# Query columns inside the z product, and a new order of the passes, in a gated cross-attention block

## What is computed

```python
# xattn(q=layernorm(x), k=ctx, v=ctx): channel mixing, 8 groups of 32 channels
t = Wt @ ctx;  p = Wp @ layernorm(x);  g = Wg @ ctx
att = sum over each group of p * g
y = Wz(group-wise) @ (att * t);  yn = (y - mean) * rsqrt(var + eps)   # per group
w = x + tanh(g_xattn) * (yn * gn_w + gn_b + ctx)
# ffn(h=layernorm(w)): 64 experts of rank 8, the best 16 of each row
q = h @ Wq.T;  scores = q @ keys.T                 # 16 query columns, 64 scores
gate = softmax of the 16 highest scores, 0 elsewhere
z = h @ A.T                                        # 512 columns
out = w + tanh(g_ffn) * 2 * ((z * gate per expert) @ B.T)
```

## Time and profile before

| | us |
|---|---|
| median of 3 runs (343.94 to 344.65) | 344.52 |
| the profiled execution, its own time | 344.88 |
| its span, first to last instruction | 343.1 |
| TensorE busy (matmul) | 335.0, 98% |
| VectorE, ScalarE, GpSimd busy | 253.6, 155.2, 155.6 |
| mean granted TensorE clock | 0.993 |

### The profile page before, as it was taken

How to read it: one execution, slowest core, us unless ns; L and a number is a source line. 1 busy time by engine, 2 the same in 40 slices (tenths; PEclk the granted TensorE clock), 3 DMA queues, 4 the chain that set the end, 5 groups by cost and what they waited for, 6 DMA issues and landing times.

```text
span 343.1 us, 5733 instructions
## 1 busy us (share of the span) xinstructions
PE 335.0 (98%) x2108; PEld 304.0 (89%) x2108; DVE 253.6 (74%) x656; ACT 155.2 (45%) x254; POOL 155.6 (45%) x148
## 2 busy tenths in 40 slices
PE   8999997999999999999999999999999999999996
PEld 8587997789988999889988899889998899889984
DVE  0858999899688866897868975888668978685362
ACT  2489826873165622554234811656225542144110
POOL 0082999189354470654445381544706544001000
PEclk9999999899999999999999999999999999999999
DMA  8999603660642509052370606424090110002002
GB/s 274 406 394 399 237 1 104 265 214 33 197 171 67 181 6 332 32 166 82 86 283 0 220 29 201 168 71 176 8 330 32 63 62 2 1 0 108 16 32 92
DMA packets 14924, 47.50 MB, mean 138 GB/s; under 512 B 1824, under 2 KB 1952, under 8 KB 14896
## 3 DMA queue, kind: packets, MB, share of 16 engines
q1 hardware_dynamic: 14544, 46.93, 38.5%
q10 hardware_dynamic: 352, 0.20, 0.2%
HBM read 38.74 MB, written 8.39 MB: 137 GB/s over the span
## 4 chain that ended last, share of the span: by engine, by line
PE 86%; POOL 9%; issue 2%; ACT 1%; DVE 1%; POOLq 0%; DVEq 0%
PE z_ps L926 24%; PE w_ps L953 24%; PE w_ps L814 10%; PE w_ps L859 10%; PE t_ps L913 4%; PE z_ps L885 3%; PE w_ps L839 2%; PE z_ps L798 2%; PE w_ps L926 2%; PE w_ps L963 2%; PE t_ps L940 2%; POOL A_lo L267 2%; POOL cT_lo L260 2%; POOL xT_lo L260 1%; POOL B_lo L267 1%
## 5 line engine op out<-in xcount | busy, mean ns | idle before, releaser
L260 POOL TENSOR_TENSOR xT_lo<-xT_in,xT_hi 128x512 fp32r<-128x512 f32 x28 | 35.6, 1295 | 48.9 <-ACT xT_hi L358 46.1
L953 PE MATMUL w_ps<-B_hi,zT_hi 128*128 128x512 f32 x128 | 53.4, 417 | 1.8 <-DVE zT_lo L653 1.8
L953 PE MATMUL w_ps<-B_hi,zT_lo 128*128 128x512 f32 x128 | 51.0, 398 | 0.0
L953 PE MATMUL w_ps<-B_lo,zT_hi 128*128 128x512 f32 x128 | 50.7, 396 | 0.0
L926 PE MATMUL z_ps<-A_hi,hT_hi 128*128 128x288 f32 x224 | 48.5, 298 | 1.0 <-DVE hT_lo L648 1.0
L926 PE MATMUL z_ps<-A_lo,hT_hi 128*128 128x288 f32 x224 | 48.0, 296 | 0.0
L926 PE MATMUL z_ps<-A_hi,hT_lo 128*128 128x288 f32 x224 | 47.9, 296 | 0.0
L437 ACT ACTIVATE ex<-sc,neg_max 128x64 f32<-128x64 f32 x16 | 5.6, 349 | 74.6 <-DVE neg_max L663 74.6
L926 PEld LDWEIGHTS z_ps<-A_hi,hT_hi 128*128 128x128 f32 x224 | 36.3, 189 | 1.8 <-DVE hT_lo L648 1.2
L926 PEld LDWEIGHTS z_ps<-A_hi,hT_lo 128*128 128x128 f32 x224 | 36.1, 189 | 0.0
L260 POOL TENSOR_TENSOR cT_lo<-cT_in,cT_hi 128x512 fp32r<-128x512 f32 x28 | 36.0, 1308 | 0.0
(11 more groups left out here) (147 smaller groups left out, 802.3 us busy)
## 6 DMA issues: line engine op xcount, KB each, us to landing
c_sb<-in_ctx SPq DMA_DIRECT2D x16, 512.0 KB, 4.9
x_sb<-in_x SPq DMA_DIRECT2D x16, 512.0 KB, 7.3
xT_in<-in_xT SPq DMA_DIRECT2D x14, 512.0 KB, 6.7
cT_in<-in_cT SPq DMA_DIRECT2D x14, 512.0 KB, 7.7
out_block<-uw SPq DMA_DIRECT2D x14, 512.0 KB, 2.7
A_in<-in_aT SPq DMA_DIRECT2D x8, 256.0 KB, 12.8
B_in<-in_bT SPq DMA_DIRECT2D x8, 256.0 KB, 12.5
xT_first<-in_xT SPq DMA_DIRECT2D x2, 512.0 KB, 9.0
```

The costliest lines, as they stand in the source:

```text
L260: last = pool.tensor_tensor(lo[:, chunks, :], came[:, chunks, :], hi[:, chunks, :].bitcast(f32), ALU.subtract)
L953: last = pe.matmul(w_ps[k][:, :], z[:, t, row], w[:, j, cols], start=(j == 0 and z is zT_hi and w is B_hi), stop=(j == KN - 1 and z is zT_lo))
```

## The change

- The 16 query columns of Wq stand behind the 512 of A (`awT`, 528 columns), so a z matmul has 264 columns. The router product, its split and the load of Wq alone go. For each tile the 16 query columns are copied (VectorE), transposed (TensorE, `queries`), copied, and multiplied with keys in fp32 into 64 scores (`scores`). In the last two chunks bank 1 of z, which holds the queries, comes before bank 0.
- The exponentials and the reciprocal in the gate are written to PSUM.
- Middle samples: z of tile 0 (with hT of tile 1 after three chunks), queries, Gram, u (tile 1 first), zT 0, z of tile 1 (with group_means), queries, N' (now in a t_ps bank), outputs (group_att_var after three chunks of output 1, zT of tile 1 after four), and hT of tile 0 between outputs 2 and 3.
- `out_product` does the passes with the high half of z first and waits for the low half only then.
- The offsets kappa go from VectorE to ScalarE; in samples 0 and 1 the variance terms of the groups too.
- The start: 12 and 4 `keep_busy` transposes in place of 24 and 8, ctx of sample 0 loaded by column halves, the w tiles of sample 0 in halves, and another split of the lots among VectorE (2, 3, 4, two of B) and GpSimd (0, 1, 5 to 7, six of B).

```diff
+        def z_banks(t, n):
+            return w_ps[NH:USES] if t == 1 and n in (0, NB - 1) else z_ps
+        def gate_space(t, n):
+            bank = z_banks(t, n)[1]
+            at = ZH + P
+            return bank[0:RD, ZH:at], bank[:, at:at + NE], bank[:, ZH:ZH + NE], bank[:, ZH + NE:ZH + NE + 1]
...
+        def u_tiles(n):
+            return range(T) if n < 1 else (1, 0)
+        def u_uses(n):
+            return [NH * t + h for t in u_tiles(n) for h in range(NH)]
...
+        def n_bank(n):
+            return z_ps[0] if n < 2 else t_ps[0]
...
+            def load_first_c():
+                for h in range(NH):
+                    cols = slice(h * HALF, (h + 1) * HALF)
+                    sp.dma_start(c_sb[0][:, :, cols],
+                                 ctx[0].rearrange("t p d -> p t d")[:, :, cols]).then_inc(c_in[h], 16)
...
@@ gpsimd @@
             x_root(0)
             x_add(0)
+            lot_low(0)
+            lot_low(1)
             y_root(0)
             pool.wait_ge(w_done, per_tile(0, T - 1))
-            for j in range(KH, KD):
+            for j in range(KH + 1, KD):
...
+            w_root(0)
             xT_low(0, 1)
-            w_root(0)
             cT_low(0, 1)
             xT_low(1, 1)
             cT_low(1, 1)
+            x_root(1)
             for j in range(KD, KD + KN):
                 lot_low(j)
-            x_root(1)
+            for j in range(KD + KN + 2, N_LOTS):
+                lot_low(j)
             x_add(1)
...
@@ scalar: sample 0, then the loop @@
             xT_high(0, 1)
             cT_high(0, 1)
-            xT_high(1, 1)
             hT_high(0, 0)
             w_square(0)
+            hT_high(1, 0)
+            u_copy(1)
+            xT_high(1, 1)
             cT_high(1, 1)
             act.wait_ge(wp_in, 16)
             act.activation(Wp_hi[:, :, :], Wp_raw[:, :, :], ACT.Copy).then_inc(wp_hi_s, 1)
-            hT_high(1, 0)
-            u_copy(1)
             exps(0, 0)
+            offsets(0)
             act.wait_ge(gram_done, per_tile(0, T - 1))
-            for j in range(KD, KD + KN):
+            for j in range(KD, N_LOTS):
                 lot_high(j)
+            scale_ctx(1)
             exps(1, 0)
             zT_high(0, 0)
             cb_copy(1)
-            scale_ctx(1)
             M_high(1)
-            for j in range(KD + KN, N_LOTS):
-                lot_high(j)
+            u_variance(1)
+            zT_high(1, 0)
             residual(0)
-            zT_high(1, 0)
-            for h in range(NH):
-                xT_high(h, 2)
-                cT_high(h, 2)
+            xT_high(0, 2)
+            cT_high(0, 2)
+            xT_high(1, 2)
+            hT_high(0, 1)
+            cT_high(1, 2)
             w_square(1)
-            hT_high(0, 1)
             hT_high(1, 1)
+            offsets(1)
...
                 zT_high(0, b)
-                exps(1, b)
+                u_copy(m)
                 if nn < NB:
                     xT_high(0, nn)
                     cT_high(0, nn)
-                u_copy(m)
+                exps(1, b)
                 zT_high(1, b)
                 if nn < NB:
                     xT_high(1, nn)
...
                 w_square(m)
                 hT_high(0, m)
                 hT_high(1, m)
+                offsets(m)
...
@@ vector @@
+            def queries(t, n):
+                dve.wait_ge(q_done, per_tile(n, t))
+                dve.tensor_copy(q_sb[:, :], z_banks(t, n)[1][:, ZH - RD:ZH]).then_inc(q_copied, 1)
+                dve.wait_ge(qT_done, per_tile(n, t))
+                dve.tensor_copy(qT_sb[:, :], gate_space(t, n)[0]).then_inc(qT_copied, 1)
...
-                step(dve.scalar_tensor_tensor(eg[:, :], sc2[:, :], TAKEN, ex[:, :], ALU.is_equal, ALU.mult,
+                step(dve.scalar_tensor_tensor(eg[:, :], sc2[:, :], TAKEN, ex, ALU.is_equal, ALU.mult,
                                               accum_out=g_sum[:, :]))
                 settle()
-                step(dve.reciprocal(g_rec[:, :], g_sum[:, :]))
-                settle()
-                step(dve.tensor_tensor(g_scale[:, :], g_rec[:, :], w_rs[:, t:t + 1], ALU.mult))
+                step(dve.reciprocal(g_rec, g_sum[:, :]))
+                settle()
+                step(dve.tensor_scalar(g_scale[:, :], g_rec, w_rs[:, t:t + 1], None, ALU.mult))
...
+            slopes(0, two_lots)
+            for k in range(NH * T - 1):
+                first_w(k)
+            hT_low(0, 0, (0,))
+            first_w(NH * T - 1)
+            hT_low(0, 0, (1,))
+            lot_low(4)
...
             for b in range(1, NB - 1):
                 m = b + 1
-                x_stats(m)
+                queries(0, b)
                 minus_means(m)
                 gate(0, b)
                 gram_fix(m)
                 M_low(m)
+                u_statistics(m, (1,))
+                x_plus_ctx(m)
+                u_statistics(m, (0,))
                 zT_low(0, b)
-                x_plus_ctx(m)
+                group_deviation(m)
+                queries(1, b)
                 gate(1, b)
-                u_statistics(m)
                 att_reduce(m)
-                group_deviation(m)
                 slopes(m, lambda: zT_low(1, b))
                 w_tiles(m)
                 add_out(0, b)
                 add_out(1, b)
+                add_out(2, b)
                 hT_low(0, m)
-                add_out(2, b)
+                add_out(3, b)
+                if m + 1 < NB:
+                    x_stats(m + 1)
                 hT_low(1, m)
-                add_out(3, b)
-                offsets(m)
+            queries(0, NB - 1)
             gate(0, NB - 1)
...
@@ tensor @@
+                    order = range(2) if k < KD - 2 else (1,)
                     for h, w in ((hT_hi, A_hi), (hT_hi, A_lo), (hT_lo, A_hi)):
-                        for i in range(2):
-                            last = pe.matmul(banks[i][:, 0:ZH], h[:, t, row], w[:, k, i * ZH:(i + 1) * ZH],
-                                             start=(k == 0 and h is hT_hi and w is A_hi),
-                                             stop=(k == KD - 1 and h is hT_lo))
-                    if gated and k == at:
-                        gated()
+                        for i in order:
+                            last = product(h, w, k, i)
+                    if k in between:
+                        between[k]()
+                last.then_inc(q_done, 1)
+                for k in range(KD - 2, KD):
+                    for h, w in ((hT_hi, A_hi), (hT_hi, A_lo), (hT_lo, A_hi)):
+                        last = product(h, w, k, 0)
                 last.then_inc(z_done, 1)
...
+            def queries(t, n):
+                pe.wait_ge(q_copied, per_tile(n, t))
+                pe.transpose(gate_space(t, n)[0], q_sb[:, :], ident[:, :]).then_inc(qT_done, 1)
+            def scores(t, n):
+                if n == 0 and t == 0:
+                    pe.wait_ge(keys_in, 16)
+                pe.wait_ge(qT_copied, per_tile(n, t))
+                pe.matmul(gate_space(t, n)[1], qT_sb[:, :], keys_sb[:, :], start=True, stop=True).then_inc(scores_done, 1)
...
-                    for z, w in ((zT_hi, B_hi), (zT_hi, B_lo), (zT_lo, B_hi)):
-                        last = pe.matmul(w_ps[k][:, :], z[:, t, row], w[:, j, cols],
-                                         start=(j == 0 and z is zT_hi and w is B_hi),
-                                         stop=(j == KN - 1 and z is zT_lo))
-                    if j == KN // 2 - 1 and middle:
-                        middle()
+                    for w in (B_hi, B_lo):
+                        pe.matmul(w_ps[k][:, :], zT_hi[:, t, row], w[:, j, cols], start=(j == 0 and w is B_hi),
+                                  stop=False)
+                    if j in between:
+                        between[j]()
+                pe.wait_ge(zT_lo_s, per_tile(n, t))
+                for j in range(KN):
+                    last = pe.matmul(w_ps[k][:, :], zT_lo[:, t, j * P:(j + 1) * P], B_hi[:, j, cols], start=False,
+                                     stop=(j == KN - 1))
                 last.then_inc(out_done, 1)
...
-            keep_busy(24)
+            keep_busy(12)
...
-            keep_busy(8)
+            keep_busy(4)
...
-            pe.wait_ge(wq_in, 16)
-            pe.wait_ge(keys_in, 16)
-            for k in range(KD):
-                last = pe.matmul(t_ps[0][:, k * NE:k * NE + NE], wq_sb[:, k * P:k * P + P], keys_sb,
-                                 start=True, stop=True)
-            last.then_inc(router_done, 1)
...
-            u_product(1, lambda: group_att_var(0))
-            pe.wait_ge(router_lo_s, 1)
+            u_product(1, {(0, T - 1): lambda: group_att_var(0)})
             hT(0, 0)
-            z_product(0, 0, z_ps, lambda: hT(1, 0), KN - 2)
-            pe.wait_ge(u_copied, per_use(1, USES - 1))
-            z_product(1, 0, w_ps[NH:USES])
+            z_product(0, 0, {2: lambda: hT(1, 0)})
+            pe.wait_ge(u_copied, u_use(1, USES - 1))
```

(56 more changed lines are left out.)

234 lines of the change are left out of this document (140 added, 94 removed).

## The result

Over 20 executions each, the changed kernel takes 344.9 us in the median (344.59 to 347.6), the kernel before 344.63 beside it (343.08 to 345.62). The ratio is 1.0031, with a 95% interval of 1.0017 to 1.0046: slower by 0.3%, where I had forecast faster by 0.5%. The time lies inside the range, the sign is wrong. The profiled execution takes 344.62 us (span 342.8), 0.3 less than that of before.

The account below looks back on a forecast made before the run. TensorE issue intervals bound the six middle samples; opening -3.45, small passes and narrow z -1.5, turn-taking +3.5, end -0.3 sum to -1.75 from 344.88: 343.1, or 342.8 us as median; range 338.6 to 346.0.

Parts of the forecast that it names:

- Narrower z: z matmuls of 264 columns in place of 288: 10.1 ns less each, 0.485 us a tile, 0.97 a sample.
- The small passes: Each tile's query transpose and fp32 score product on TensorE: 0.35 us a tile added, bounds 0.25 and 0.60.
- rival (c): The small passes cost 0.6 us a tile, 4 us more over 16 tiles, 346.8; chance with the rest 0.08.
- The turn-taking: GpSimd's xT_low piece between VectorE's two w tiles delays hT_lo; z waits 0.7 us in five middle samples, +3.5.
- (a): Turn-taking costs z nothing, as GpSimd's pieces come later or fit behind both w tiles: 339.3 us; chance 0.28.
- (b): GpSimd gets in ahead of the first w tile, one more 1.25 us piece in five samples: 349.1 us; chance 0.14.
- The first middle sample: GpSimd's c_lo comes some 0.5 us late for u, as its queue started later: +0.5.
- The opening: Shorter warm-up, clock, samples 0 and 1, and late c_lo: -1.8 + 0.7 - 2.85 + 0.5 = -3.45 us.
- wait of N' for M_lo: Samples 0 and 1: M_lo stands behind a lot on VectorE, so N' waits 0.5 us.
- y's root: Samples 0 and 1: y's root stands behind two more lots on GpSimd, which just fits.
- fall of the clock: Some 2 us of idle before N' of sample 0 may bring 1.2 GHz; 1.7 us at under even odds, counted 0.7.
- The end: Narrow z saves 0.25 us, a wait of 0.2 before output 2 goes, queries add about 0.15: -0.3.

Follow-up runs that it names:

- what padding gave back: Changed kernel with queries and keys padded with zeros to 128 rows: 341.03 to 341.64 us at full clock, ratio 0.9933 to the kernel before.
- the experiment that takes it away: Changed kernel with xT's second half rounded later, behind hT_high: 341.77 to 342.44 us at full clock, ratio 0.9964 to the kernel before.

## Why the prediction was wrong

**Narrower z: right.** 48 matmuls take 5.9 us, about 123 ns each as forecast; 0.485 a tile is won.

**The small passes: the step that failed.** I took 0.35 a tile, with 0.60 as the upper bound; it is 0.11 + 0.55 = 0.66. The transpose was right. The score product was sized by the group product, whose weights have 128 rows; mine have 16. I had chosen the nearest row by the count of passes and of columns, when what matters was the shape of the weights, and the trace of before did hold loads of 16 rows, the router's, though only in a row of their own (16 loads of 16 rows one behind the other, at 23.25). Net, a tile costs 0.17 more where I had 0.13 less, so 16 tiles are 2.7 us dearer in place of 2.1 cheaper. By itself that is 4.8 us of forecast gone, or 3.4 by what padding gave back. It was my rival (c), whose price of 4 us was nearly right and whose chance, with the rest, I put at 0.08. Of the terms that I had wrong this one decides the sign: with 128 rows the kernel is 0.7% faster than before. (Without the wait on hT_lo, which I had in the sum, it is 0.4% faster too.)

The Trainium skill (TensorE: Matmul & The Clock Gate, section "The mechanism") says that "LDWEIGHTS overlaps with in-flight MATMULs only when row_grp differs". Here 128-row loads begin while a 128-row matmul runs, on the same rows (the load at 76.59 beside a matmul that starts at 76.59), so the sentence does not hold as it stands; the same section also lets a load go ahead into "the background weight buffer", which would fit these. The 16-row and 64-row loads do wait, and for that no run here shows the reason.

**The turn-taking: mechanism and place right, size somewhat below.** Two w tiles 3.52 (3.7 forecast), one piece of GpSimd between them, a wait on hT_lo in just the five samples named. It costs 0.45 by the starts and 0.53 by the experiment that takes it away, against 0.7 (bounds 0.4 and 1.0): 2.7 us in place of 3.5. Rivals (a) and (b) fall: the wait is there, and GpSimd comes second, by 0.20 us. With the rule of the Trainium skill (SBUF — State Buffer, section "SBUF: two separate sides"), an exclusive lock for a whole instruction, the trace agrees: with no GpSimd piece beside them the tiles are back to 2.48.

**The first middle sample: wrong by nearly its half microsecond.** I had c_lo late for u by 0.5. A weight load of u does wait for it, but the matmul behind comes only 0.07 late (83.55 to 83.85 in place of 0.23), and the sample takes 110.00 - 69.28 = 40.72, like the others.

**The opening: right in sum, in part by luck.** The first fp32 product starts at 6.58 (forecast 6.9, and 8.73 before), N' of sample 0 waits 1.84 ("some 2 us of idle"), and nothing waits for zT_lo. I took ctx to be there by then; it is only just: the product waits 0.4 for it here, and 0.7 to 1.0 where the variants start it at 6.76 to 6.87. The wait of N' for M_lo (0.5 forecast) is not there. But y's root, which I had as just fitting, stands behind GpSimd's additions until 63.33, VectorE waits 2.74 for it, and the transposes of w wait 0.85 where they had waited 0.34. The two errors cancel. The warm-up's rate is read from durations alone: its 12 transposes take 2.66 us, 0.22 each against 0.11 later, while the profile gives the granted clock there as 1.00. z of sample 1 comes 4.6 earlier; I had 4.65 without a fall of the clock and 3.95 with 0.7 for it. The narrow z of sample 0 cost 0.3 there instead of saving it, so the rest was 0.5 better than said. The clock's fall is real: 2.2 us in 12 of 31 executions, 0.85 on the mean, and 0.2 in the median of the first twenty (344.90 for 344.71).

**The end: -0.3 forecast, +0.25 measured.** Two tiles' small passes are 0.6 of it, the step that failed once more.

**The sum** in the profiled execution: -0.3 for -1.75. The difference of 1.45 is -0.65 in the opening, +1.55 in the middle (with its wait taken away a sample is 40.18 against 239.84 / 6 = 39.97, so 0.21 longer where I had 0.25 shorter, 2.8 over six; the wait is 0.8 less and c_lo 0.4 to 0.5; by the rows of the small passes alone it would be 0.33 longer, and that tenth is unexplained) and +0.55 at the end. The medians then stand the other way round, since the profiled execution of before was 0.25 above its median and that of after 0.3 below.

The forecast was right that two gains in the opening and a new wait would nearly cancel. With a result so near zero, an error of 0.3 us in a step that is done 16 times decides the sign, and the range said so better than the chances did: 0.20 for slower was too little for a sum whose largest unmeasured term had no row of its own shape.

## What to carry to other kernels

Size a small product by a row whose weights have the same number of rows: in a dense stream of 128-row matmuls one with 16 or 64 costs 0.55 us in place of 0.22, and padding with zeros to 128 rows brings it back to 0.22. When a step is moved nearer to the next sample, follow the SBUF-reading instructions of VectorE and GpSimd through the stretch; two that meet take turns, and the cure is to move the one nobody waits for. And read the granted clock of every execution: a median over two groups hides what either kernel costs at full clock.

## What the runs showed of the hardware

A weight load of 16 or of 64 rows behind matmuls of 128 rows is not taken ahead, nor the load behind it: 0.09 before the product, 0.36 for two passes of 64 columns, 0.10 behind, the same for both sizes within 0.01. A transpose with 128 rows and 16 columns of weights, in the same stream, costs 0.11 and no more.

VectorE and GpSimd take turns in the w tiles, whose operands lie in SBUF: two take 2.48 with no GpSimd piece beside them, and the second alone takes 2.32 when it has to wait for one. The three output additions behind it, with one operand in PSUM, take 2.06 beside GpSimd's second piece, 0.69 each, and lose nothing.

An idle of 1.84 us on TensorE, in a stretch that is otherwise dense, is followed in 12 of 31 executions by some microseconds at 1.2 GHz, and in the others by none. Sixteen transposes of the identity in it, free in themselves, end that.
